# A transformer layer on one Trainium2 core: who subtracts the query-key remainders, and the step orders of all five queues

## What is computed

```python
def _L0_attn_ref(x, W_Q, b_Q, W_K, b_K, W_V, b_V, W_O, b_O):
    Q = jnp.einsum('btd,hkd->bthk', x, W_Q) + b_Q
    K = jnp.einsum('btd,hkd->bthk', x, W_K) + b_K
    V = jnp.einsum('btd,hkd->bthk', x, W_V) + b_V
    scores = jnp.einsum('bqhk,bshk->bhqs', Q, K) / jnp.sqrt(jnp.asarray(d_head, x.dtype))
    attn = jax.nn.softmax(scores, axis=-1)
    out_h = jnp.einsum('bhqs,bshk->bqhk', attn, V)
    return jnp.einsum('bqhk,hdk->bqd', out_h, W_O) + b_O
...
x = x + _layernorm(_L0_attn_ref(_layernorm(x, axis=-1), ...), axis=-1)
x = x + _layernorm(_L0_ffn_ref(_layernorm(x, axis=-1), ...), axis=-1)
```

## Time and profile before

| | |
|---|---|
| median of 3 runs | 979.77 us (979.45 to 981.7) |
| the profiled execution's own time | 980.0 us |
| its span | 978.2 us |
| PE, PEld | 98%, 79% busy |
| DVE, ACT, POOL | 93%, 91%, 78% busy |
| granted TensorE clock | 0.993 of full speed |

### The profile page before, as it was taken

The page is one execution under the profiler, slowest core; times in us unless marked ns, Lnnn a source line. Parts: engine busy times, 40 slices in busy tenths (PEclk is TensorE's granted clock), DMA queues, the critical chain, the costliest instruction groups (busy, mean ns, idle before and its releaser), DMA issues.

```text
span 978.2 us, 28088 instructions
## 1 busy us (share of the span) xinstructions
PE 960.1 (98%) x8582; PEld 773.8 (79%) x8582; DVE 909.9 (93%) x1666; ACT 887.7 (91%) x3183; POOL 759.9 (78%) x746
## 2 busy tenths in 40 slices
PE   8999999999999999999999999999999999999995
PEld 7777888778888878888877888877888887888874
DVE  6999999999999999999999999999999999999972
ACT  4999999999999999999999999999999999999872
POOL 2777988888888788878878878887888878877862
PEclk9999999999999999999999999999999999999997
DMA  7276775666676666676666676666677666667560
GB/s 267 53 164 139 172 163 135 142 151 138 157 172 140 138 151 138 145 177 146 138 152 138 139 172 159 137 145 146 138 161 169 139 137 153 138 149 173 136 145 11
DMA packets 58467, 143.32 MB, mean 147 GB/s; under 512 B 16960, under 2 KB 25664, under 8 KB 58432
## 3 DMA queue, kind: packets, MB, share of 16 engines
q1 hardware_dynamic: 58432, 142.89, 63.2%
HBM read 6.50 MB, written 4.19 MB: 11 GB/s over the span
## 4 chain that ended last, share of the span: by engine, by line
PE 93%; DVE 2%; SPq 2%; ACT 1%; issue 1%; DMA 0%; POOL 0%; POOLq 0%; DVEq 0%; ACTq 0%
PE o_ps L487 24%; PE st_ps L462 21%; PE extra_ps L521 9%; PE qk_ps L428 6%; PE qk_ps L429 6%; PE qk_ps L430 6%; PE xv_ps L442 4%; PE extra_ps L358 3%; PE xv_ps L444 3%; PE xv_ps L443 3%; PE extra_ps L543 2%; SPq L313 2%; PE extra_ps L556 2%; PE extra_ps L558 1%; PE xv_ps L358 1%
## 5 line engine op out<-in xcount | busy, mean ns | idle before, releaser
L1795 POOL TENSOR_TENSOR probs<-probs,inv_sum 128x1024 f32<-128x1024 f32 x256 | 484.4, 1896 | 115.2 <-DVE inv_sum L1315 108.0
L850 ACT ACTIVATE probs<-st_ps,neg_max 128x256 f32<-128x256 f32 x1024 | 476.9, 496 | 33.7 <-DVE neg_max L1307 31.8
L1307 DVE TENSOR_REDUCE neg_max<-st_ps 128x4 f32<-128x1024 f32 x256 | 308.6, 1206 | 11.3 <-PE st_ps L462 10.5
L1326 DVE STREAM_TRANSPOSE probs_b<-probs 128x1024 f32<-128x1024 f32 x252 | 309.2, 1230 | 1.1 <-POOL probs L1795 1.1
L487 PE MATMUL o_ps<-probs_t,v_sb 128*64 128x256 f32 x2048 | 249.3, 385 | 1.2 <-DVE o_lo L1341 0.7
L850 ACT ACTIVATION_READ_ACCUMULATOR probs<-st_ps,neg_max 128x1 f32 x1024 | 231.5, 226 | 0.0
L487 PEld LDWEIGHTS o_ps<-probs_t,v_sb 128*64 128x64 f32 x2048 | 135.8, 136 | 80.8 <-DVE o_lo L1341 10.4
L462 PE MATMUL st_ps<-qk_hi 64*128 64x256 f32 x1024 | 162.7, 314 | 1.6 <-ACT probs L850 0.9
L836 ACT CAST qk_hi<-qk_ps 128x512 fp32r<-128x512 f32 x256 | 153.2, 599 | 11.1 <-PE qk_ps L430 6.2
L462 PE MATMUL st_ps<-qk_lo,qk_hi 64*128 64x256 f32 x1024 | 145.3, 279 | 0.0
L462 PE MATMUL st_ps<-qk_hi,qk_lo 64*128 64x256 f32 x1024 | 144.8, 278 | 0.0
(11 more groups left out here) (140 smaller groups left out, 1946.7 us busy)
## 6 DMA issues: line engine op xcount, KB each, us to landing
probs_t<-probs_b SPq DMA_DIRECT2D x1008, 128.0 KB, 2.4
out<-x_all SPq DMA_DIRECT2D x31, 128.0 KB, 1.9
x_all<-in_x SPq DMA_DIRECT2D x1, 3840.0 KB, 17.9
probs_b<-in_w_v SPq DMA_DIRECT2D x1, 512.0 KB, 4.2
probs_b<-in_w_o SPq DMA_DIRECT2D x1, 512.0 KB, 6.6
probs_b<-in_w_q SPq DMA_DIRECT2D x1, 384.0 KB, 5.0
probs_b<-in_w_k SPq DMA_DIRECT2D x1, 384.0 KB, 5.8
x_all<-in_x SPq DMA_DIRECT2D x2, 128.0 KB, 3.1
```

Of the source, the lines that this page charges most:

```text
L850: last = nc.scalar.activation(probs[n][:, h, j, :], st_ps[p % 2][:, (2 * h + j) * T:(2 * h + j + 1) * T], ACT.Exp, bias=neg_max[n][:, h, j ...
L1307: nc.vector.tensor_reduce(neg_max[p % N_PROBS][:, :, :].rearrange("p h j -> p (h j)"), st_ps[p % 2][:, :].rearrange("p (j s) -> p j s", j= ...
L1326: nc.vector.transpose(probs_b[chunk % 2][:, :, :, 2 * NT * n:2 * NT * (n + 1), :].rearrange("p i t n q -> p n t i q"), probs[p % N_PROBS][ ...
L1795: nc.gpsimd.tensor_tensor(probs[n][:, :, :, :].rearrange("p h j s -> p (h j) s"), probs[n][:, :, :, :].rearrange("p h j s -> p (h j) s"), ...
```

## The change

`POOL_LO` becomes `(3,)`: GpSimd does the remainder of pair 3, VectorE the other seven. With it go 32 of 64 `qk_full` copies on ScalarE and 32 of 64 subtractions on GpSimd, and 32 are added on VectorE. All five queues get newly written orders; the steps themselves are as they were, except that two of four one-element copies (`settle`) outside the loop are gone. The core of the difference (the start and the end of each queue are rewritten in the same manner):

```diff
-POOL_LO = (1, 5,)
+POOL_LO = (3,)
...
@@ sync
-            store(0)
             move_blocks(3, 0)
             move_blocks(3, 1)
+            store(0)
...
@@ tensor, the body
+                project_qk(i - 1, 7, 1 - r)
                 scores(i - 1, 5)
...
                 project_qk(i, 0, r)
+                scores(i - 1, 6)
                 probs_v(i - 2, 4, r)
...
                 scores(i - 1, 7)
-                scores(i, 0)
-                transpose_u(i - 3, free=(u_ready, i - 2))
...
@@ scalar, the body
-                qk_full(i, 1)
...
+                qk_full(i, 3)
...
-                qk_full(i, 5)
```

More of the change, by code:

```diff
@@ L587, in _ @@
             weight_means(4)
-            project_qk(0, 1, 0)
             weight_means(5)
             scores(0, 0)
+            project_qk(0, 1, 0)
             value_sums()
             project_qk(0, 2, 0)
-            project_v(0, 1, 0, free=(v_copied[0], 1))
             scores(0, 1)
@@ L596, in _ @@
             scores(0, 2)
-            project_v(0, 2, 0, free=(v_copied[1], 1))
+            project_v(0, 1, 0, free=(v_copied[0], 1))
             project_qk(0, 4, 0)
             scores(0, 3)
-            project_v(0, 3, 0, free=(v_copied[2], 1))
+            project_v(0, 2, 0, free=(v_copied[1], 1))
             project_qk(0, 5, 0)
             scores(0, 4)
+            project_qk(0, 6, 0)
+            project_v(0, 3, 0, free=(v_copied[2], 1))
+            scores(0, 5)
             transpose_xn(1, free=(v_copied[3], 1))
-            project_qk(0, 6, 0)
+            project_qk(0, 7, 0)
@@ L625, in _ @@
+            probs_v(0, 2, 0)
             project_qk(1, 6, 1)
-            probs_v(0, 0, 0)
-            probs_v(0, 1, 0)
-            scores(1, 4)
+            scores(1, 5)
+            probs_v(0, 3, 0)
             project_qk(1, 7, 1)
[L630 to L634, removed]
             scores(1, 6)
-            project_qk(2, 1, 0)
-            project_v(2, 1, 0, free=(v_copied[0], 3))
@@ L638, in _ @@
             probs_v(0, 4, 0)
             probs_v(0, 5, 0)
+            project_qk(2, 0, 0)
+            project_v(2, 0, 0, free=(xt_lo_ready, 3))
             scores(1, 7)
-            project_qk(2, 2, 0)
             ffn_means()
+            project_qk(2, 1, 0)
             scores(2, 0)
@@ L645, in _ @@
             probs_v(0, 7, 0)
+            project_qk(2, 2, 0)
             scores(2, 1)
+            project_v(2, 1, 0, free=(v_copied[0], 3))
             project_qk(2, 3, 0)
-            project_v(2, 2, 0, free=(v_copied[1], 3))
             output_projection(0)
@@ L744, in _ @@
             project_qk(31, 0, 1)
-            scores(30, 7)
+            scores(30, 6)
             probs_v(29, 4, 1)
             probs_v(29, 5, 1)
+            project_qk(31, 1, 1)
+            scores(30, 7)
+            project_v(31, 1, 1, free=(v_copied[0], 32))
+            project_qk(31, 2, 1)
             transpose_u(28, free=(u_ready, 29))
[L749 to L752, removed]
             probs_v(29, 6, 1)
             probs_v(29, 7, 1)
+            project_z(28, free=(ut_ready, 29))
+            project_v(31, 2, 1, free=(v_copied[1], 32))
+            scores(31, 0)
             scores(31, 1)
-            project_v(31, 1, 1, free=(v_copied[0], 32))
             project_qk(31, 3, 1)
@@ L760, in _ @@
             scores(31, 2)
-            scores(31, 3)
+            probs_v(30, 0, 0)
+            probs_v(30, 1, 0)
             transpose_y(29, free=(yt_ready, 30))
             project_qk(31, 5, 1)
[L764 to L769, removed]
+            scores(31, 3)
             probs_v(30, 2, 0)
             probs_v(30, 3, 0)
+            transpose_x1(29, free=(x1_ready, 30))
+            scores(31, 4)
             project_tg(29, free=(x1t_ready, 30))
             project_v(31, 3, 1, free=(v_copied[2], 32))
-            project_qk(31, 7, 1)
+            project_qk(31, 6, 1)
             scores(31, 5)
-            scores(31, 6)
             probs_v(30, 4, 0)
@@ L779, in _ @@
             transpose_u(29, free=(u_ready, 30))
-            transpose_last(4, 1)
-            transpose_last(4, 0)
+            project_qk(31, 7, 1)
+            scores(31, 6)
             project_z(29, free=(ut_ready, 30))
@@ L1423, in _ @@
             weight_lo("k", late, w_hi_ready, w_lo_ready)
+            qk_lo(0, 1)
             row_max(0, 0)
```

813 lines of the change are left out of this document (404 added, 409 removed).

## The result

The changed kernel takes 989.43 us in the median of 4 runs (988.66 to 991.14), the kernel before, run beside it, 979.61. The ratio is 1.0094, with an interval of 1.0080 to 1.0108: slower by 0.9%, where 989.0 was forecast. The profiled execution is the longest of the four, with a span of 989.3 us and a time of 991.14. So the two profiled spans differ by 11.1 us and the medians by 9.8.

A forecast was written before the change was run, and what follows sets the result against it. TensorE's own list was taken to bound each round: +8.4 us in the loop and +0.6 outside, the rest at 0, sum +9.0 on 980.0, giving 989.0 us. Its own range was 984.5 to 993.5, the overall range 982 to 997.

The forecast's parts named there:

- TensorE sets the pace in the loop: Loop: a round lasts as long as TensorE's own list, busy for all 29.05 and 29.09 us at full clock.
- The entry costs 0.19 us and is no wait: TensorE, from projection into scores: first two distances 0.43 us, not 0.12 each, costing 0.19 whatever the projection's lead.
- A round costs +0.31: Loop body: seven entries into scores instead of five, other neighbours changed; +0.31 us a round, +8.4 us over 27 rounds.
- the term for the other neighbours: TensorE's loop list: changed neighbourhoods other than entries into scores give back 0.07 us a round, -1.9 us in all.
- The start and the end, taken as 0: Outside the loop: smoother start up to -6.4 us, as much again the other way; 0 taken between.
- VectorE's remainder is hidden, with 0.7 us left: Loop: one more remainder adds 0.60 us, giving VectorE 28.6 to 28.7, under the new round's 29.4.
- ScalarE and GpSimd at nothing: Loop: one bank copy and one 1284 ns subtraction fewer per item, priced at nothing since both engines waited before.
- VectorE or the hand-off: Rival: VectorE, or bank `qk_ps` between pairs 2 and 3 with 0.09 us left, becomes the bound; 996 us, chance 0.20.
- A smoother start: Rival: less GpSimd and ScalarE work and other lists remove most of the start's 6.4 us; 982.6 to 984, chance 0.13.
- Every change of mode at one price: Rival: TensorE's mode changes, 588 instead of 527, each cost at least 0.09 us; +5.5 us, 985.5, chance 0.04.
- A wait in disguise: Rival: the entry's 0.19 us is held-up weight loads that longer leads remove; -11 us, 969, chance 0.05.
- half of the bound at the start either way: Reason given for the forecast's own range, 984.5 to 993.5; the bound at the start was 6.4 us.

The follow-up runs named there:

- e4: Kernel before, only pair 5's remainder moved from GpSimd to VectorE, TensorE's list untouched: 993.24 us, ratio 1.0152.
- e9: Changed kernel with pair 0's remainder also given to GpSimd, so VectorE has six again, TensorE's new list kept: 998.47 us, ratio 1.0192.
- e5: Kernel before, TensorE's scores of pair 3 moved ahead of pair 5's projection, ScalarE's copy of pair 5's bank moved later: 990.01 us, ratio 1.0111.
- e6: Kernel before, scores of pairs 3 and 1 moved ahead of projections of pairs 5 and 3, ScalarE's and VectorE's lists fitted: 998.94 us, ratio 1.0204.
- e8: Kernel before, pair 5's remainder given to VectorE, pair 6's remainder and x1 moved ahead of pair 2's block transpose there: 998.88 us, ratio 1.0206.
- e3: Kernel before, scores of pair 5 put next to pair 6's on TensorE, pair 5's row maximum moved on VectorE: 1046.18 us, ratio 1.0686.
- e1: Kernel before, only TensorE's body list changed, scores of pair 3 moved ahead of pair 5's projection: 1001.57 us, ratio 1.0239.
- e7: Changed kernel with pair 7's remainder also given to GpSimd, so VectorE has six again, TensorE's new list kept: 1008.20 us, ratio 1.0296.

## Why the prediction was right, and where its steps were off

**TensorE sets the pace in the loop.** Right, but not for the reason given first. That TensorE is busy for the whole round proves little, as e4's round of 29.30 shows. What bears it out is e9: with VectorE's seventh remainder taken away the distances of TensorE's list stay, and so does the round. "In 27 rounds TensorE is never late" was wrong by 0.05 us in every second round, ahead of qk7.

**The entry costs 0.19 us and is no wait.** Right. The two distances are 0.21 and 0.22 us at all seven entries after, and at those that e5 and e6 add, behind `output_projection` and `project_z`. No lead of the operands changes them. In e5 and e6 each entry comes with a way out to a projection that costs 0.19 more; in the change the ways out to full-array steps are three before and after, so only the entries count.

**A round costs +0.31.** The sign and the count of entries were right, the size was 0.235: the term for the other neighbours should have been -0.145 and was -0.07. The sum took x1 ahead of qk7 at the old loop's own distance. That held a wait for pair 6's remainder (738 ns on average), and the new list has 704: some 0.03, which I had counted as the price of standing there. The rest is a few nanoseconds in each of many blocks (a scores block behind a projection 905 instead of 912, one behind another 714 instead of 720, the output projection 2867 instead of 2879). The three neighbourhoods that the old trace did not have came out at 572, 578 and 576 ns for the assumed 580. So the loop cost 6.3, or 6.7 with the one longer round, where +8.4 was forecast.

**The start and the end, taken as 0.** Wrong by what made the sum come out: about +3 us in the medians (9.8 less the loop's 6.7, as profiled), where the sum had +0.6 for three entries. In the profiled execution TensorE is idle for 4.3 us between 11.4 and 97.4 instead of 2.4, and the clock was at its lower level in two stretches, 3.41 us each from 21.58 and 38.65, where the kernel before had one, from 35.41. In a stretch at the lower level matmuls start 0.43 us apart in place of 0.23, so it costs about half its length, an estimate of 1.7 us. Idle time and clock, 1.9 and 1.7, account for the start's 3.4 us within 0.2. Ahead of its two stretches TensorE had stood still for 0.65 us (up to 16.5), and for 0.42, 0.22 and 0.30 (up to 29.0, 31.8 and 33.1). In the kernel before it was 0.17 and 0.12 (up to 26.4 and 30.0); of the 14 held-up loads that the prediction names as what went ahead of that stretch, 11 came after it. The four runs' mean clock was 0.994 and 0.993 at 988.66 and 989.01, 0.990 at 989.85 and 991.14. This goes along with the time, but it also holds the lower clock of the last part, so it doesn't count the stretches.

So the forecast of 989.0 lies within 0.4 us by luck: 1.7 too much in the loop, about 2.5 too little outside, and 0.4 too much in the value before that it was added to. The waits of TensorE's matmuls from 10 to 120 us say what was late at the start; after:
```profile
PE qk_ps L428 <- DVE qk_lo L1296: 1.4, 4, 0.5
PE o_ps L487 <- DVE o_lo L1335: 1.1, 2, 0.8
```
Before, the first was 0.5 us in 2 times and the second isn't there. So, by the releasers that the profile names, it is VectorE's work, which the prediction had named as the reason for the other end of its bound (VectorE "has more to do just there") and then set against the relief of ScalarE and GpSimd at zero. Whether the seventh remainder or only the new order makes it late was not tried.

**VectorE's remainder is hidden, with 0.7 us left.** It came true, and the reason given was too weak. 28.6 us of 29.4 is no cover: e4 has as much work on VectorE in the old lists, with 0.7 to 0.9 us idle, and loses 0.32 us a round. What hides it is where the computed lists put it.

**ScalarE and GpSimd at nothing.** Right in the loop: relieved by 0.5 to 0.6 and 1.2 to 1.7 us a round, they wait longer (GpSimd for VectorE 91.5 us, 73.2 before).

**The rivals.** *VectorE or the hand-off*: not here. The bank between pairs 2 and 3 was free 0.20 us early, not 0.09, as both engines stood waiting for it: 1.34 us was needed. The 1.47 of the earlier trace rows was not read with both engines ready, since VectorE was still at the two instructions ahead:
```profile
423.60 0.69 DVE L1341 TENSOR_TENSOR o_lo<-o_ps,o_hi 128x512 fp32r<-128x512 f32 x1
424.20 0.17 DVE L1315 RECIPROCAL inv_sum<-row_sum 128x4 f32<-128x4 f32 x1
```
Of the 0.20 some 0.06 is the delay that a waiting matmul has as well, so 0.14 was to spare. But the mechanism is real in this kernel, as e4, e8 and e3 show. *A smoother start*: the start became rougher. *Every change of mode at one price*: at the smallest price, 0.09 us, e5's two more changes would be 0.18 a round; it has 0.34. *A wait in disguise*: the leads grew and the entries kept 0.21 and 0.22.

One number of the forecast doesn't follow from its own terms: "half of the bound at the start either way" would be half of 6.4 us, 985.8 to 992.2, and not 984.5 to 993.5. Both hold the measured 989.43.

## What to carry to other kernels

Where one engine is busy for the whole round, the order of its own list is a cost: count how often it enters and leaves a kind of step that is dearer to enter, before counting work taken off its neighbours. Idle share on a second engine says nothing of whether one more instruction there is free; look for the next step whose result is awaited, how much it was early, and take off what a waiting step has too (here 0.06 us early, all of it such a delay: nothing to spare). And that the first engine reads as busy throughout doesn't show that it never waits; compare distances from start to start. And an experiment that moves one engine's steps in a kernel with lists in order must move the partners' steps too, or it measures their misfit: e1 and e5 have the same TensorE list and differ by 11.6 us.

## What was not expected of the hardware

Leaving a block of scores (halves of 64 rows) for a full-array projection costs as much as entering one, 0.21 and 0.22 us for the first two distances, so a block that is entered and left by projections costs 0.38 more than one that joins another. A matmul that waited for VectorE starts 0.06 us after that instruction ends (e4), and one that waited for ScalarE's exponentials 0.145 us after (e7). And within the first 80 us of the program the lower clock was granted for a while in every profiled execution: for 3.41 us in that of the kernel before, and for 3.41 twice in that of the changed one, each time behind the short standstills given above. Its mean over a run, 0.990 to 0.994 in four runs of the changed kernel, differs from launch to launch of the same program.
